# Counts of a token routing formed over tiles by fifteen more products, and the subtractions of GpSimd moved away from VectorE's, in a two-layer attention and mixture kernel

## The reference

```python
# mixture: every token to the expert of its highest logit, and a shared network for all
logits = x @ w_router.T
_, top_idx = jax.lax.top_k(logits, 1)
mask = jax.nn.one_hot(top_idx, 16).sum(axis=1)
scores = jax.nn.sigmoid(logits) * mask
gate, up = split(einsum('eth,ehf->etf', scores.T[:, :, None] * x[None], gate_up_proj))
expert_out = einsum('etf,efh->eth', up * silu(gate), down_proj)
out = silu(x @ w_gate.T) * (x @ w_up.T) @ w_down.T + expert_out.sum(axis=0)
# choice: every expert takes its k best tokens of each batch
affinity = softmax(einsum('bsd,ed->bse', x, gate_w)).transpose(0, 2, 1)
gating, idx = jax.lax.top_k(affinity, 64)
x_e = (silu(x_in @ w_gate.T) * (x_in @ w_up.T)) @ w_down.T      # x_in = x[idx]
out = zeros.at[idx].add(gating * x_e)
```

## Time and profile before

| what | us |
|---|---|
| median of 3 runs | 1582.4 (1577.87 to 1582.47) |
| the profiled execution | 1578.58 |
| its span, first to last instruction | 1576.9 |
| busy: TensorE matmul, VectorE, ScalarE, GpSimd | 1454.4, 946.8, 883.6, 651.6 |
| TensorE's granted clock, mean | 0.966 |

### The profile page before, as it was taken

How to read it: one execution, slowest core, us unless ns; L and a number is a source line. 1 busy time by engine, 2 the same in 40 slices (tenths; PEclk the granted TensorE clock), 3 DMA queues, 4 the chain that set the end, 5 groups by cost and what they waited for, 6 DMA issues and landing times. The chain is left out here.

```text
span 1576.9 us, 28767 instructions
## 1 busy us (share of the span) xinstructions
PE 1454.4 (92%) x10026; PEld 1198.4 (76%) x10026; DVE 946.8 (60%) x1762; ACT 883.6 (56%) x2198; POOL 651.6 (41%) x956
## 2 busy tenths in 40 slices
PE   7999999999999999969899999899997569999995
PEld 5878787878787878748789988676665248888885
DVE  4776767676767676746411114888888644444542
ACT  4886878777867687734311113676774224444442
POOL 7514444444343433050511003546321035877774
PEclk8999999999999999979999999899999779999998
DMA  5400000000000000010589993100000513444442
GB/s 173 138 2 21 1 22 1 18 6 1 21 2 21 2 1 1 1 32 3 204 297 315 318 316 93 28 14 17 13 1 2 166 54 109 125 121 125 123 114 27
DMA packets 74449, 120.29 MB, mean 76 GB/s; under 512 B 7008, under 2 KB 55136, under 8 KB 74304
## 3 DMA queue, kind: packets, MB, share of 16 engines
q1 hardware_dynamic: 63600, 101.76, 19.8%
q0 software_dynamic: 10704, 16.65, 5.2%
HBM read 99.78 MB, written 18.61 MB: 75 GB/s over the span
## 5 line engine op out<-in xcount | busy, mean ns | idle before, releaser
L519 ACT ACTIVATE a_p<-a_s,a_negmax 128x512 f32<-128x512 f32 x256 | 176.2, 688 | 110.4 <-DVE a_negmax L647 61.0
L647 DVE TENSOR_REDUCE a_negmax<-a_s 128x1 f32<-128x512 f32 x256 | 176.3, 689 | 74.6 <-PE a_s L380 70.7
L279 POOL TENSOR_TENSOR a_o_l<-a_o,a_o_h 128x256 fp32r<-128x256 f32 x64 | 47.0, 736 | 296.9 <-ACT a_o_h L544 296.9
L389 PEld LDWEIGHTS a_t<-ident,a_p 128*128 128x128 f32 x1024 | 122.4, 140 | 50.7 <-issue 22.8
L389 PE MATMUL a_t<-ident,a_p 128*128 128x128 f32 x1024 | 157.0, 276 | 0.7 <-DVE a_pT L662 0.7
L1708 ACT ACTIVATE h_probs<-h_scores,h_negmax 128x256 f32<-128x256 f32 x256 | 118.2, 478 | 65.8 <-DVE h_negmax L1898 65.8
L2203 POOL TENSOR_TENSOR n_w_l<-n_raw,n_w_h 128x768 fp32r<-128x768 f32 x64 | 118.2, 1847 | 74.4 <-ACT n_w_h L2246 74.4
L407 PE MATMUL a_out_p<-a_pT,a_v 128*64 128x256 f32 x1024 | 124.6, 385 | 0.0
L379 PE MATMUL a_s<-a_k_hl,a_q_hh 128*128 128x512 f32 x256 | 105.9, 414 | 2.3 <-issue 1.5
L2385 DVE TENSOR_TENSOR n_hidden<-n_up,n_silu 128x512 f32<-128x512 f32 x64 | 44.3, 693 | 98.3 <-PE n_up L2288 94.0
L380 PE MATMUL a_s<-a_k_hl,a_q_l 128*128 128x512 f32 x256 | 100.5, 393 | 0.0
(11 more groups left out here) (436 smaller groups left out, 4444.8 us busy)
## 6 DMA issues: line engine op xcount, KB each, us to landing
e_w_in<-in_L_ffn_gate_up_proj SPq DMA_DIRECT2D x31, 1024.0 KB, 6.9
n_raw<-in_L_ffn_w SPq DMA_DIRECT2D x64, 384.0 KB, 3.0
e_w_out<-in_L_ffn_down_proj SPq DMA_DIRECT2D x31, 512.0 KB, 5.4
rows_in<-a_zeros SPq DMA_DIRECT2D x1, 3968.0 KB, 15.2
e_rows<-rows_in SPq DMA_DIRECT2D x31, 128.0 KB, 5.1
rows_out<-spare POOLq DMA_DIRECT2D x31, 128.0 KB, 4.5
a_both<-in_ctx SPq DMA_DIRECT2D x8, 256.0 KB, 2.7
a_both<-in_x SPq DMA_DIRECT2D x8, 256.0 KB, 3.0
```

Source lines behind the costliest of these rows:

```text
L389: ins = pe.transpose(turned_p[j % 2][:, c, :], probs[j][:, c * P:(c + 1) * P], g.ident[:, :])
L519: act.activation(probs[j][:, :], scores[j % 2][:, :], ACT.Exp, bias=negmax[:, j:j + 1], accum_out=total[:, r % 2, j % 2, j // 2:j // 2 + 1 ...
L647: dve.tensor_reduce(negmax[:, j:j + 1], scores[j % 2][:, :], AX.X, ALU.max, negate=True).then_inc(max_set, 1)
```

## The change

Four edits. TensorE's `count` adds fifteen products that sum over the earlier tiles in the accumulator, so VectorE's doubling steps go. VectorE's `route` has three parts instead of four, and `scale_queries` moves from unit 8 to unit 6, ScalarE's `w_h` from units 8 to 11 to units 7 to 10. GpSimd waits for low(11), the last of the early units, ahead of its four subtractions. In the choice, VectorE makes the rests of chunks 0 and 1 once the list is written, and GpSimd begins with chunk 2.

```diff
@@ gpsimd, mixture, behind the 16 scatters
+                pool.wait_ge(low, EARLY)
                 for n, (high_w, low_w) in enumerate(splits):
                     pool.wait_ge(wh_set, n + 1)
                     pool.tensor_tensor(low_w[:, :, :], raw[n], high_w[:, :, :], ALU.subtract).then_inc(wl_set, 1)
@@ tensor, count()
-                    pe.matmul(count_ps, before_w[:, :], hot_b[:, :, :], start=True, stop=True)
-                    pe.matmul(total_ps, ones_w[:, :], hot_b[:, :, :], start=True, stop=True).then_inc(counted, 1)
+                    pe.matmul(total_ps, ones_w[:, :], hot_b[:, :, :], start=True, stop=True)
+
+                    pe.matmul(count_ps, before_w[:, :], hot_b[:, :, :], start=True, stop=False)
+                    for back in range(1, NT):
+                        ins = pe.matmul(count_ps[:, back:NT, :], ones_w[:, :], hot_b[:, 0:NT - back, :],
+                                        start=False, stop=(back == NT - 1))
+                    ins.then_inc(counted, 1)
@@ scalar
-                    elif n >= 8:
-                        if n == 8:
+                    elif n >= 7:
+                        if n == 7:
                             act.wait_ge(raw_set, 1)
-                        if n - 8 < len(splits):
-                            act.activation(splits[n - 8][0][:, :, :], raw[n - 8], ACT.Copy).then_inc(wh_set, 1)
+                        if n - 7 < len(splits):
+                            act.activation(splits[n - 7][0][:, :, :], raw[n - 7], ACT.Copy).then_inc(wh_set, 1)
@@ vector, route(part)
-                        dve.tensor_copy(within[:, :, :], count_ps)
-                        dve.tensor_copy(tile_sum[:, :, :], total_ps)
-                        link(dve.tensor_copy(sums[0][:, :, :], total_ps))
-                        running(sums, lambda a, i, j: a[:, i:j, :], NT)
-                    elif part == 2:
-                        link(dve.tensor_tensor(within[:, :, :], within[:, :, :], tile_sum[:, :, :], ALU.subtract))
-                        link(dve.tensor_tensor(within[:, :, :], within[:, :, :], upto[:, :, :], ALU.add))
-                        link(dve.tensor_scalar(padded[:, :], upto[:, NT - 1, :], float(P - 1), None, ALU.add))
+                        link(dve.tensor_reduce(tile_sum[:, 0, :], total_ps.rearrange("p t e -> p e t"), AX.X, ALU.add))
+                        link(dve.tensor_scalar(padded[:, :], tile_sum[:, 0, :], float(P - 1), None, ALU.add))
...
-                    elif part == 3:
-                        link(dve.tensor_tensor(within[:, :, :], within[:, :, :], over(starts[:, :], NT), ALU.add))
+                    elif part == 2:
+                        link(dve.tensor_tensor(within[:, :, :], count_ps, over(starts[:, :], NT), ALU.add))
...
-                    elif part == 4:
+                    elif part == 3:
@@ vector, the units
-                    if n in range(3, 7):
+                    if n in range(3, 6):
                         route(n - 2)
-                    elif n == 8:
+                    if n == 6:
                         scale_queries()
@@ gpsimd, choice
-                low_w(0)
-                low_w(1)
                 pool.wait_ge(listed, 1)
...
+                            if c == 0:
+                                pool.wait_ge(wl_set, 2)
                             low_w(c + 2)
@@ vector, choice, behind the list
+                for c in range(2):
+                    dve.wait_ge(wh_set, c + 1)
+                    dve.tensor_tensor(w_l[c][:, :], raw[c][:, :], w_h[c][:, :], ALU.subtract).then_inc(wl_set, 1)
                 low_rows(0)
```

More of the change, by code:

```diff
@@ L828, in run_mixture @@
         before_w, ones_w = sb("r_before_w", [P, P], BF16), sb("r_ones_w", [P, P], BF16)
-        within, sums = sb("r_within", [P, NT, E]), [sb(f"r_sums{i}", [P, NT, E]) for i in range(2)]
+        within = sb("r_within", [P, NT, E])
         tile_sum = sb("r_tile_sum", [P, NT, E])
@@ L1316, in running @@
                     return bufs[src]
-                upto, end = sums[(NT - 1).bit_length() % 2], ends[(E - 1).bit_length() % 2]
+                end = ends[(E - 1).bit_length() % 2]
                 def route(part):
@@ L1509, in _ @@
                     shared(n)
+                    if n % FC == 0 and n > EARLY:
+                        add(n // FC - 1)
                 low_x(0)
```

## The result

The changed kernel took 1569.36 us (median of 7 executions, 1568.49 to 1579.03), the kernel before 1582.72 beside it (7 executions). The ratio is 0.9925, 95% interval 0.9900 to 0.9951: faster by 13 us, between 8 and 16, which is under 1% of the time. The profiled execution after was the longest of its seven, 1579.03 us with a span of 1577.3.

A forecast was written before the change was run, and what follows sets the result against it. TensorE was taken to bound the early units of the mixture, VectorE alone the choice until the list is written. Gains of 5.8 (mixture) and 2.0 (choice), 7.8 us, against the median 1582.4 gave 1574.6 us; range 1569 to 1580.

The forecast's parts named there:

- The gain of the choice is 2.0.: Choice: the polynomial gains 2.9 us, VectorE's subtractions holding GpSimd's gathers cost 0.9; net 2.0, between 1.3 and 2.9.
- By columns they cost 0.8 us, by instructions 1.65. I take 1.2.: Mixture: cost of TensorE's fifteen added products, 1.2 us, covered by the waits of 0.9 and 0.6 behind them.
- I take 0 for up(11).: Mixture: net shift of TensorE's last early up product, 0 us, between −0.4 and +0.5.
- A hold ... 3.6 us of it.: Mixture, kernel before: GpSimd's subtractions hold VectorE's low(10) for 3.6 us of its 4.32.
- They end with the scatters: Mixture, chosen case: TensorE's late signals end with GpSimd's scatters, 5.1 us earlier, so the experts start at 776.0.
- G 5.8: G is how much earlier the expert blocks start; 5.8 us in the chosen case.
- rival 1: Mixture: the late signals vanish, as fewer scatters meet the second weights; 6.8 and 2.0, 8.8 us gained, chance 0.2.
- A start that is G earlier should carry to the end.: Expert blocks to the kernel's end: everything behind the start follows it, so the full G is gained.
- Block 3's weights: Expert blocks: the splits moved behind low(11) don't delay the fourth weights, with 0.7 us to spare.
- Rival 3: Gathers held the full 1.6 us, block 3's weights 2 us late: some 1.3 us gained in all, chance 0.12.
- Rival 4: Mixture: earlier scatters meet the first weights, causing a second spell of late signals; 5.4 us slower, chance 0.05.

The follow-up runs named there:

- the routing alone: The changed kernel without GpSimd's wait and with the choice as before (fifteen products, shorter route, ScalarE's halves a tile earlier): 1575.93 us, ratio 0.9965 to the kernel before.
- set 5: Runs together on one chip: both edits 1583.5 us; GpSimd's wait plus ScalarE's halves earlier 1577.0; changed kernel waiting for one rest less 1583.68; before 1580.19.
- both edits: Changed kernel with weights of blocks 1 and 2 sent for earlier and VectorE's two choice subtractions behind the gathers: 1583.5 us, and 1568.52 us when repeated unchanged.
- sets 2, 3, 4 and 6: Groups run together: changed kernel (1569.36 us); parts of the change; changed kernel and before again plus each small edit singly; both edits repeated (1568.52 us).

## Why the prediction was right, and where it was not

The forecast was 1574.6 us, and 1569.36 came, inside the range but only 0.4 above its low end of 1569. That it came so near is in part luck: the case of the mixture that I chose was the wrong one, and a set like the fifth could have put the time above the range. By its steps:

- **"The gain of the choice is 2.0."** Right. The polynomial took 2.25 us (2.3 expected), the stretch to `t_token` shrank by 2.9, and the hold on the gathers gave back 0.8 (0.9 taken; 0.59 of it in the first gather, between 1.05 and 1.64). It was one hold, not one for each subtraction: the three other gathers took 0.95 to 0.96 us. The Trainium skill's rule in "SBUF — State Buffer", section "Who interferes with whom", was read in the prediction as saying that the gathers would not be held. They are, 1.64 against 1.05 us for the same gather. That does not refute the page: its inference is about the writing of descriptors alone, and a gather also reads its list `t_token` from SBUF, where the rule's other half, on GpSimd's reads, would have it held. Which of the two parts was held no row shows.
- **"By columns they cost 0.8 us, by instructions 1.65. I take 1.2."** The gate product behind the counts starts at 735.55, not 734.86, and TensorE came to the counts 0.25 us earlier (734.47 for their first product, 734.72 before), so they cost 0.9. Covered, as argued. TensorE's rows after, for this point and the next:

```profile
734.69 1.01 PE L1086 MATMUL m_small<-r_hot_b,r_ones_w 128*128 128x240 bf16 x15
735.55 0.48 PE L1014 MATMUL m_gate<-xT_h,shared_h 128*128 128x512 f32 x1
...
767.56 0.39 PE L1014 MATMUL m_up<-xT_h,shared_l 128*128 128x512 f32 x1
```

- **"I take 0 for up(11)."** Too cautious. Its last product starts at 767.56, 1.3 us earlier than the 768.87 of the earlier trace rows, since TensorE does not wait at all on the way there, and `r_top` is 0.3 us earlier. That is a gain of 1.0, outside the bounds of −0.4 to +0.5.
- **"A hold ... 3.6 us of it."** Mis-sized. Where signals are on time it is 5.2 us, through all four subtractions, and TensorE waits 6.0 us behind it with nothing else late. In the first profile `out_l` came 2.4 us behind the others only since ScalarE was late, so three subtractions held low(10), and the late hidden(10) made up the rest. The prediction also took down's products at 0.12 us each without a word on the clock. Behind a wait of 6 us they took 0.21 at first (776.03 to 776.24 us), and in all six profiles in which TensorE waited 4.6 us or more there, the granted clock fell to the lower level, during the wait or just after it, for 6.8 or 10.2 us; in the other eight it stayed at 1.00 up to the experts.
- **"They end with the scatters", G 5.8.** This step failed. I took the late signals for a part of the schedule, because the one trace had them. In both profiles of the change they were gone, as in rival 1 (G 6.8); with the 1.0 of up(11) that makes 7.8. 7.7 came out, and the sum with the choice is 9.8 instead of 7.8. Rival 1 had the right case for a reason that did not hold: the kernel before, too, has no late signals in its second profile.
- **"A start that is G earlier should carry to the end."** It does. 7.7 and 2.1 make 9.8 against 1582.4: 1572.6. The ratio's interval holds it (0.62% in 0.49 to 1.00), and the two sets with the change gave 13.4 and 11.9 between medians. What lies above 9.8 I can't place. The choice, the wait and the routing alone gained 2.4, 5.5 and 5.4 us by the medians, close to the 1.8, 6.0 and 6.1 of their stages. Every kernel whose experts start at 42.1 gained 1.2 to 3.6 us more than its stages, which no single interval tells from nothing. The median of the mean granted clock was 0.966 for the kernel before and 0.970 for the changed one. A part of that is the fall behind the long wait, but the kernels with the wait or the routing alone have no such fall either, and nothing above their stages.
- **Block 3's weights**, with "0.7 us to spare": they went out 3.9 us behind the experts' start, no later than before, so the moved splits did not hold them up. Rival 3 fell.
- **Rival 4, slower, by late signals that meet the scatters earlier.** In the two sets of the change itself it fell, but in set 5 something of its kind happened. Two kernels that differ from the change by small edits started their experts 11.2 and 13.4 us later than 42.1, and took 0.2% more than before. Its price was 5.4 us. The changed kernel itself has not been seen in such a set; that it would lose there is likely from these two, not shown.

Why late signals cost nothing before and up to 13.4 us after follows from the rows only in part. Before, TensorE waited 6.0 us for the hold anyway, its scatters began at 749.7, and signals were seen late from 763.7 on. With both edits in set 5 the scatters began at 744.6, and the signal of 754.57 is late already, while more of the shared tiles are still to come. What makes the signals late in one set and not in another stays open.

## What to carry to other kernels

Before a wait that one trace shows is put into a sum, look whether it is in a second trace of the same kernel: here a spell of late signals in one of two profiles of the kernel before hid the true size of the hold, and the same kind of spell turned one kernel from faster to slower than before between two sets. Two edits that remove the same wait don't add (6.0 and 6.1 gave 7.7), so time each alone before keeping both. In this kernel a subtraction of GpSimd's belongs where VectorE has nothing on the path, and back-to-back ones are best counted as one long hold. A long wait of TensorE's costs more than its length: price the products behind it at the clock that the rows show there.

## What the runs showed of the hardware

- One kernel had two times, 1583.5 and 1568.52 us, on different occasions, each stable over its executions. In the longer one TensorE's signals reached ScalarE 9.9 and VectorE 11.4 us late while GpSimd issued indirect scatters and 297 GB/s were moving. The same scatters and the same 297 GB/s stand in the shorter one, without late signals. All three kernels profiled in that set had them, the kernel before in its first profile, and none of the ten in sets 2, 3, 4 and 6.
- VectorE's instruction was held to the end of GpSimd's fourth subtraction (5.86 us in two profiles, 4.49 in one that began later in the row, instead of 0.69), from one to the next, and in another profile it got in ahead of the fourth.
- The second attention has two lengths, about 219 us (11 of 14 profiles) and about 228 (two), with one at 224.0, and the long ones have the lower granted clock (0.93 against 0.98, and 0.95 in the one between), in kernels that do the same work there. One profile's span can be 9 us off by this. Why the clock fell more in one execution than in another of the same kernel no row says.
- During or just after a wait of TensorE's of 4.6 to 9.0 us in the mixture the granted clock fell to its lower level in six of six profiles, for 6.8 or 10.2 us. Twelve products of 256 columns took 2.7 us there and 1.4 at the upper level.
